# Sorting groups of 4096 edges by merged runs, with row scaling on ScalarE and one-comparison one-hots, in a three-pass graph kernel

## The chip, the cores and the metric

The kernel runs on one core of a Trainium2 chip. The metric is the device time of one execution in microseconds (us), smaller is better. TensorE (PE) multiplies, VectorE (DVE) and ScalarE (ACT) work elementwise, GpSimd (POOL) issues the gathers, SyncE (SP) issues the plain transfers.

## The reference

`x` has 12500 nodes of 96 features; 200000 edges (`src`, `dst`, `weight`, 32 attributes) are sorted by `dst`. A GCN of two layers and one GINE layer follow each other:

```python
# gcn_conv, twice: out[d] = sum over edges (s, d) of norm * (h @ W)[s]
norm = dinv[row] * ew * dinv[col]
out = jax.ops.segment_sum(h[row] * norm[:, None], col, num_segments=n_nodes)
x = x + log_softmax(gcn2(relu(gcn1(relu(layernorm(x))))))
# GINE: message, sum by target, small MLP, batch norm
msg = jax.nn.relu(x[src] + edge_attr @ We + be)
aggr = jax.ops.segment_sum(msg, dst, num_segments=x.shape[0])
```

So there are three passes over all edges (passes 0, 1, 2). Each fetches a row of 96 floats per edge by `src` and adds the rows up by `dst`; passes 0 and 1 weigh each row by the edge's weight, pass 2 adds the attributes' term and takes a ReLU.

## The kernel before, in words

**Steps.** 512 edges (4 per partition, G = 4) are a step; there are NS = 391. Step s uses buffer u = s mod 10 (U = 10), and a loop iteration has 10 steps: 38 iterations (LOOPS) and 11 last steps. A step in pass 0 is: ACT stages the edge's indices and weights (`stage`), POOL issues four gathers of 128 rows from a table in HBM into `rows_g` (`gather`, line 658), DVE makes a one-hot of the targets (`build_hot`: for each of the four columns, `iota == target` times the weight, 128 wide), PE multiplies rows by one-hot into PSUM (`aggregate`, line 1142), and DVE adds the window of 128 nodes into `acc` (`add_window`, line 1582). ACT stages step s + 10 once step s is aggregated.

**Selected rows.** In passes 1 and 2 steps 3, 5, 7, 9 of an iteration (SEL) have no gather. Their edges were sorted by block (`src` mod 100) during pass 0, in groups of 2048 edges, one group per iteration. PE then picks the rows out of a table in SBUF (`tab3`, three bfloat16 parts of 96, so 288 columns): a sorted column of 128 edges spans at most KB = 10 blocks, so `select` multiplies ten `mask`s by ten table columns for each of four columns, 40 matmuls (line 1222). DVE makes the masks (line 1605) and sums the three parts into `rows_g` (`join_rows`, line 1619). Of an iteration's 40 gathers 24 are left. The iteration runs in four segments: `select(i)`, then the aggregations of SEGS[i]. In pass 2 the gathered steps also take an edge term: PE turns the attributes (line 1124) and multiplies them (line 1129), DVE adds (line 1591), ACT takes the ReLU (line 890).

**The sort in pass 0.** For a group of 2048 edges PE and DVE count blocks and ranks (lines 1150 to 1158, 1641 to 1658), DVE makes a permutation `iota_h == rank` of 128x2048 for each of the 16 columns (line 1662), and PE multiplies each by the attributes and the payload in four matmuls of 512 columns (line 1165). These lie in steps 2 to 7 between the aggregations; each engine takes its instructions in the order in which they are written, and waits on semaphores.

## Time and profile before

| | |
|---|---|
| median of 3 runs | 5602.56 us (5595.03 to 5612.93) |
| profiled execution | 5616.2 us, its span 5614.4 us |
| pass 0 | 270 to 2435 us |
| pass 1 | 2541 to 3794 us |
| pass 2 | 3971 to 5455 us |
| mean granted clock of TensorE | 0.855 |
| busy | PE 77%, POOL 67%, DVE 66%, ACT 23% |

The passes' limits are the first gather, the last aggregation and the first and last `select` in the trace. Busy shares are means over passes with different limits, so each pass is read by itself. A DMA_INDIRECT row of POOL is the making of one gather's descriptors. Rows give busy time of a group, the mean length of one instruction, and the engine's idle time before it with what ended it.

### The profile page before, as it was taken

To read this page: it belongs to the slowest core of one execution; us is meant where nothing else is said; L and a number is where in the kernel's file an instruction comes from. 1 tells how busy PE (TensorE), PEld (TensorE's weight loads), DVE (VectorE), ACT (ScalarE), POOL (GpSimd) and SP (SyncE) were. 2 spreads that over 40 slices of the span, in tenths; PEclk is the share of its full clock that TensorE was granted. 3 is DMA by queue.
4 is the path that set the end of the run, shared out by engine and by line. 5 is a ranking of instruction groups with operands and counts; after the bars stand their busy time and mean duration, and the time that the engine had idled before them with its cause. 6 is when DMAs were issued, how large, how long until landed. Compare 5 with 4: busy or idle time off the path is not lost.

```text
span 5614.4 us, 116632 instructions
## 1 busy us (share of the span) xinstructions
PE 4328.9 (77%) x29893; PEld 3358.6 (60%) x29894; DVE 3689.5 (66%) x10748; ACT 1292.0 (23%) x4287; POOL 3768.6 (67%) x3554
## 2 busy tenths in 40 slices
PE   4566666666666666668999999996699999999995
PEld 4444444444444444456777777775577777777773
DVE  3466666665666666647888888886666666666662
ACT  5111111111111111142111111113433333332223
POOL 2377777777777777737777777775666665666663
PEclk6577787777778787859999999996899999999997
DMA  2122222222222222212222222223232322222224
GB/s 54 37 47 46 50 47 47 48 47 48 46 48 46 49 48 49 46 52 52 52 51 51 51 51 51 51 48 111 65 70 65 70 68 66 70 62 67 63 59 109
DMA packets 239972, 316.92 MB, mean 56 GB/s; under 512 B 69263, under 2 KB 175178, under 8 KB 239545
## 3 DMA queue, kind: packets, MB, share of 16 engines
q0 software_dynamic: 111232, 170.85, 15.6%
q1 hardware_dynamic: 128688, 145.48, 8.9%
q8 instruction: 20, 0.33, 0.0%
q14 instruction: 32, 0.26, 0.0%
HBM read 276.92 MB, written 39.15 MB: 56 GB/s over the span
## 4 chain that ended last, share of the span: by engine, by line
PE 60%; DVE 13%; POOL 11%; issue 10%; DVEq 2%; ACT 2%; DMA 1%; POOLq 0%; ACTq 0%; SPq 0%
PE psum L1222 26%; PE psum L1142 15%; POOL rows_g L658 11%; PE psum L1165 7%; PE psum L1129 3%; DVE x_tab L1662 2%; PE psum L1086 2%; PE psum L1150 2%; PE psum L1154 1%; DVE x_tab L1657 1%; DVEq L432 1%; PE psum L1214 1%; PE psum L1289 1%; DMA rows_g<-table,idx 1%; DVE rows_g L1619 1%
## 5 line engine op out<-in xcount | busy, mean ns | idle before, releaser
L658 POOL DMA_INDIRECT rows_g<-table,idx x3476 | 3605.6, 1037 | 1547.3 <-issue 1011.3
L1222 PE MATMUL psum<-x_tab 125*128 x8512 | 1148.9, 289 | 83.9 <-issue 46.2
L1142 PE MATMUL psum<-hot,rows_g 128*96 128x128 f32 x7512 | 1077.4, 297 | 143.5 <-DMA rows_g<-table,idx 70.7
L1142 PEld LDWEIGHTS psum<-hot,rows_g 128*96 128x96 f32 x7512 | 980.8, 181 | 236.4 <-issue 145.8
L1222 PEld LDWEIGHTS psum<-x_tab 125*128 125x128 bf16 x8512 | 827.3, 97 | 393.9 <-issue 135.0
L1165 PE MATMUL psum<-x_tab 128*104 128x512 bf16 x2432 | 614.5, 403 | 534.4 <-DVE x_tab L1662 526.3
L1582 DVE TENSOR_TENSOR acc<-acc,psum 96x128 f32 x1173 | 328.8, 280 | 962.9 <-PE psum L1142 945.2
L791 ACT ACTIVATE attr<-edge 128x12 f32 (+1 forms) x1173 | 243.5, 211 | 2806.3 <-PE psum L1142 2805.6
L1165 PEld LDWEIGHTS psum<-x_tab 128*104 128x104 bf16 x2432 | 303.1, 133 | 780.6 <-ACT x_tab L848 321.9
L1573 DVE TENSOR_SCALAR hot<-iota,attr 128x128 f32<-128x128 f32 x2504 | 686.4, 356 | 7.3 <-ACT acc L785 4.8
L1619 DVE TENSOR_REDUCE rows_g<-psum 128x384 f32<-128x1152 f32 x304 | 412.3, 1356 | 341.2 <-PE psum L1222 336.9
L1605 DVE TENSOR_SCALAR x_tab<-x_tab 125x512 bf16<-125x512 bf16 x2128 | 498.9, 303 | 86.3 <-ACT x_tab L810 43.3
L1222 PE MATMUL psum<-x_tab,x_more 125*128 x3648 | 493.9, 287 | 0.0
L1222 PEld LDWEIGHTS psum<-x_tab,x_more 125*128 125x128 bf16 x3648 | 353.3, 97 | 127.4 <-issue 17.1
L1662 DVE TENSOR_SCALAR x_tab<-x_tab 128x2048 bf16<-128x2048 f16 x608 | 428.1, 755 | 0.2 <-issue 0.2
L890 ACT ACTIVATE rows_g<-rows_g 128x384 f32<-128x384 f32 x391 | 201.1, 514 | 375.5 <-DVE rows_g L1619 211.6
L1142 PE MATMUL psum<-x_more,rows_g 128*96 128x128 f32 x1872 | 258.0, 282 | 27.2 <-DMA rows_g<-table,idx 15.1
L1142 PEld LDWEIGHTS psum<-x_more,rows_g 128*96 128x96 f32 x1872 | 221.5, 166 | 49.6 <-ACT rows_g L890 17.9
L1129 PE MATMUL psum<-we_blk,x_more 128*128 128x384 f32 x478 | 205.4, 512 | 57.2 <-DVE rows_g L1591 56.6
L810 ACT ACTIVATE x_tab<-x_tab,down 125x512 bf16<-125x512 uint16 x304 | 218.6, 719 | 29.8 <-issue 14.8
L1605 DVE TENSOR_SCALAR x_more<-x_tab 125x512 bf16<-125x512 bf16 x912 | 214.1, 300 | 0.0
L1569 DVE TENSOR_TENSOR hot<-iota,attr 128x512 f32<-128x512 f32 x313 | 202.1, 683 | 9.5 <-ACT idx L793 8.4
(255 smaller groups left out, 3692.3 us busy)
## 6 DMA issues: line engine op xcount, KB each, us to landing
rows_g<-table,idx POOLq DMA_INDIRECT x3476, 2.5
x_tab<-sorted_keys SPq DMA_DIRECT2D x304, 125.0 KB
x_more<-in_edge_attr_dram SPq DMA_DIRECT2D x238, 64.0 KB
sorted_attr<-x_tab SPq DMA_DIRECT2D x38, 384.0 KB
x_more<-sorted_attr SPq DMA_DIRECT2D x152, 96.0 KB
table<-x_tab SPq DMA_DIRECT2D x13, 840.0 KB
x_tab<-in_edge_attr_dram SPq DMA_DIRECT2D x38, 256.0 KB, 2.8
x_tab<-in_x_dram SPq DMA_DIRECT2D x2, 4200.0 KB
```

Of the source, the lines that this page charges most:

```text
L658: pool.indirect_dma_start(out=rows_g[u][0:np_, g * F:(g + 1) * F], out_offset=None, in_=table[p], in_offset=bass.IndirectOffsetOnAxis(ap=i ...
L791: last = act.activation(attr[u][0:np_, :], e[:, G:4 * G], ACT.Copy)
L810: act.activation(key_b[i % 2], key_in[i % 2], ACT.Identity, bias=down[0:PN, 0:1]).then_inc(s_kb, 1)
L1129: pe.matmul(ps_e[0:np_, :], eaT[:, 0:np_], we_blk[:, :], start=True, stop=True).then_inc(ring.lin, 1)
L1142: last = pe.matmul(ps_agg[t.b], rows_g[t.u][0:t.np_, g * F:(g + 1) * F], hot[t.h][0:t.np_, g, :], start=g == 0, stop=g == G - 1)
L1165: last = pe.matmul(ps_perm[b], ship[:, c, :], perm[c % 3][:, b * BK:(b + 1) * BK], start=c == 0, stop=c == SC - 1)
L1222: last = pe.matmul(ps_sel[c], mask[i % 2][j][:, c * P:(c + 1) * P], tab3[:, j:J - KB + 1 + j, :, :][:, bass.ds(w[c], 1), :, :].rearrange(" ...
L1573: last = dve.tensor_scalar(hot[t.h][0:np_, g, :], iota[0:np_, 0:W], rel[:, g:g + 1], attr[t.u][0:np_, G + g:G + g + 1], ALU.is_equal, ALU. ...
L1582: dve.tensor_tensor(a, a, ps_agg[t.b], ALU.add).then_inc(fast.added, 1)
L1605: dve.tensor_scalar(mask[i % 2][j], key_b[i % 2], float(j), None, ALU.is_equal).then_inc(s_mask, 1)
L1619: dve.tensor_reduce(rows_g[t.u].rearrange("e (c f) -> e c f", c=G), ps_sel4.rearrange("e c (k f) -> e c f k", k=3), AX.X, ALU.add).then_in ...
L1662: dve.tensor_scalar(perm[c % 3], iota_h, rank[:, c:c + 1], None, ALU.is_equal).then_inc(s_perm, 1)
```

## The change

- **Groups of 4096 edges.** Two iterations (20 steps) sort one group. Its 32 columns are four runs of eight. A run is sorted by 8 permutations of 128x1024, each used as stationary operand by eight matmuls (`permute`); the sorted runs are copied by ACT and then merged by 32 further comparisons of 128x1024, each moved through PE in two matmuls (`merge`). A sorted column then spans at most KB = 6 blocks: `select` has 24 matmuls, and six masks are made for it.
- **Paced permutations.** POOL counts `fast.issue` up before every gather of pass 0; permutation m of step k waits until gather 4 (k + 2) + m is about to be issued.
- **Wider windows.** The targets of a group of 4096 span more nodes: one-hot, aggregation and window of selected steps are 200 wide (WP), 128 for the others.
- **Weights.** In passes 0 and 1 ACT multiplies the rows in place by the weight (`scale_rows`), and the aggregation waits for that.
- **One-hots.** One `tensor_tensor` comparison makes all four columns; in passes 0 and 1 its `iota` lies in PSUM.
- In passes 1 and 2 most one-hots are written behind `join_rows`, and the edge terms stand at other blocks (`EA_AT`). The buffers of one-hots are laid out anew (`hot`, `hot_age`). Ranks of four runs come from one PSUM tile and are split into place and run rank by integer steps (`sort_rank`; a group of 4096 has 25 instructions chained by waits on DVE, a group of 2048 had 13). A branch taken only if a group doesn't fit its window puts the unsorted edges back.

```diff
+    L2, U2, N2, C2, S2 = LOOPS // 2, 2 * U, 2 * NP, 2 * SC, 2 * SE
+    NR = 4
+    RL = C2 // NR
+    RW = RL * P
+    MARGIN = 256
+    MW = NR * P + 2 * MARGIN
+    PT = 4
+    KB = 6
+    WP = 200
+    HP = 4
+    LEAD = 8
...
+            def hot(self, p):
+                if p == 0:
+                    return hot[self.h]
+                if self.sel:
+                    return hot_p[self.i]
+                return (hot_p[0], hot_g[2], hot_p[3] if p == 1 else hot_g[0])[(self.s - LOOPS * U) % 3] if self.rest else hot_g[GAT.index(self.u) % 3]
+
+            def hot_age(self, p):
+                return H if p == 0 else U if self.sel else 3 if self.rest else NG - 2
+
+            def width(self, p):
+                return WP if self.selected(p) else W
+
+            def bank(self, p):
+                return (ps_agg_p if self.selected(p) else ps_agg)[self.b]
...
             def gather(ring, p, s, u, np_, got):
                 pool.wait_ge(ring.staged, p * NS + s + 1)
-                pool.sem_inc(ring.issue, 1)
                 for g in range(G):
+                    if g == 0 or p == 0 and ring is fast:
+                        pool.sem_inc(ring.issue, 1)
...
+            def scale_rows(p, t):
+                if t.selected(p):
+                    act.wait_ge(s_row, t.pi + 2)
+                else:
+                    act.wait_ge(fast_got[t.u], t.got(p))
+                for g in range(G):
+                    r = rows_g[t.u][0:t.np_, g * F:(g + 1) * F]
+                    last = act.activation(r, r, ACT.Copy, scale=attr[t.u][0:t.np_, G + g:G + g + 1])
+                last.then_inc(s_scaled, 1)
...
             def select_pass():
                 def one(it):
                     for i in range(NP):
                         key_ahead(1, it, i)
+                        for k in SEGS[i]:
+                            scale_rows(1, Step(it, k))
                         stage_seg(1, it, i)
...
+                scale_rows(0, Step(0, 0))
+                with act.Fori(0, L2) as it:
+                    for k in range(U2):
                         sort_part(it, k)
-                        stage_fast(0, Step(it, k + U))
+                        scale_rows(0, Step(2 * it, k + 1))
+                        stage_fast(0, Step(2 * it, k + U))
...
-                elif t.selected(p):
-                    pe.wait_ge(s_row, t.pi + 2)
                 else:
-                    pe.wait_ge(fast_got[t.u], t.got(p))
+                    pe.wait_ge(s_scaled, n + 1)
                 for g in range(G):
-                    last = pe.matmul(ps_agg[t.b], rows_g[t.u][0:t.np_, g * F:(g + 1) * F], hot[t.h][0:t.np_, g, :],
+                    last = pe.matmul(t.bank(p), rows_g[t.u][0:t.np_, g * F:(g + 1) * F],
+                                     t.hot(p)[0:t.np_, g, 0:t.width(p)],
...
-                for b in range(4):
-                    last = pe.matmul(ps_perm[b], ship[:, c, :], perm[c % 3][:, b * BK:(b + 1) * BK], start=c == 0, stop=c == SC - 1)
+                    pe.wait_ge(s_keyc, it + 1)
+                if k == 0:
+                    pe.wait_ge(s_run, it * 2 * NR + 2 * r + 1)
+                    for b in range(2):
+                        pe.matmul(bank[4 + b][:, 0:HP * PM], zeros[:, 0:P], zeros[:, 0:HP * PM], start=True, stop=False)
+                pe.wait_ge(s_perm, n + 1)
+                for o in range(RL):
+                    last = pe.matmul(ps_run[o // HP][:, o % HP, :], perm[c % PT][:, o * P:(o + 1) * P], ship[:, c, :],
+                                     start=False, stop=k == RL - 1 and o % HP == HP - 1)
                 last.then_inc(s_permd, 1)
...
+            def merge(it, k, r):
+
+                n = it * 2 * C2 + C2 + k * NR + r
+                t, c = perm[(k * NR + r) % PT], ship2[:, r * RL + k, 0:PF]
+                lo = MARGIN if k == 0 else 0
+                hi = MW - MARGIN if k == RL - 1 else MW
+                if k == 0 and r == 0:
+                    pe.wait_ge(s_run, it * 2 * NR + 2 * NR + 1)
+                if r == 0:
+                    pe.wait_ge(s_eao, it * (RL + 1) + k + 1)
+                pe.wait_ge(s_perm, n + 1)
+                pe.matmul(ps_merge[k % 2][:, lo:BK], c, t[:, lo:BK], start=k == 0 and r == 0, stop=r == NR - 1)
+                pe.matmul(ps_merge[(k + 1) % 2][:, 0:hi - BK], c, t[:, BK:hi], start=r == 0,
+                          stop=k == RL - 1 and r == NR - 1).then_inc(s_permd, 1)
...
-            EA_AT = ({2: 0, 5: 1, 8: 2}, {5: 3}, {5: 4}, {5: 5})
+            EA_AT = ({1: 0, 3: 1, 5: 2}, {3: 3}, {3: 4}, {3: 5})
...
                 dve.wait_ge(fast.staged, n + 1)
-                dve.wait_ge(fast.agg, n + 1 + U - H)
+                dve.wait_ge(fast.agg, n + 1 + U - t.hot_age(p))
                 rel = attr[t.u][0:np_, 0:G]
-                if p == 2:
-                    last = dve.tensor_tensor(hot[t.h][0:np_, :, :], iota[0:np_, 0:W].unsqueeze(1).to_broadcast([np_, G, W]),
-                                             rel.unsqueeze(2).to_broadcast([np_, G, W]), ALU.is_equal)
-                else:
-                    for g in range(G):
-                        last = dve.tensor_scalar(hot[t.h][0:np_, g, :], iota[0:np_, 0:W], rel[:, g:g + 1],
-                                                 attr[t.u][0:np_, G + g:G + g + 1], ALU.is_equal, ALU.mult)
+                last = dve.tensor_tensor(h[0:np_, :, 0:w], (iota if p == 2 else ps_iota)[0:np_, 0:w].unsqueeze(1).to_broadcast([np_, G, w]),
+                                         rel.unsqueeze(2).to_broadcast([np_, G, w]), ALU.is_equal)
                 last.then_inc(fast.hot, 1)
...
-            def sort_perm(it, c):
-                dve.wait_ge(s_permd, SC * it + c + 1)
-                dve.tensor_scalar(perm[c % 3], iota_h, rank[:, c:c + 1], None, ALU.is_equal).then_inc(s_perm, 1)
...
+            def sort_perm(it, k, m):
+                q = (k - PERM_AT) * NR + m
+                dve.wait_ge(s_permd, it * 2 * C2 + q + 1)
+                dve.wait_ge(fast.issue, (it * U2 + k) * G + LEAD + m + 1)
+                if k < MERGE_AT:
+                    at = rank[:, q:q + 1]
+                else:
+                    at = place[:, m * RL + k - MERGE_AT:m * RL + k - MERGE_AT + 1]
+                dve.tensor_scalar(perm[q % PT], iota_h, at, None, ALU.is_equal).then_inc(s_perm, 1)
...
+                with dve.Fori(0, L2) as it:
                     links[0] = 0
-                    w = windows(dve, mybir.EngineType.DVE, it * U, U, win_row)
-                    for k in range(U):
+                    for k in range(U2):
+                        if k % U == 0:
+                            w = windows(dve, mybir.EngineType.DVE, it * U2 + k, U, win_row)
+                        now, ahead = Step(2 * it, k), Step(2 * it, k + LA)
                         if k == 0:
                             sort_blocks(it)
-                        build_hot(0, Step(it, k + LA))
-                        if k == 9:
+                        if PERM_AT <= k < MERGE_AT + RL:
+                            if k == MERGE_AT:
+                                sort_places(it)
+                            sort_perm(it, k, 0)
+                            if k > PERM_AT:
+                                add_window(0, Step(2 * it, k - 1), at)
+                            sort_perm(it, k, 1)
+                            build_hot(0, ahead)
+                            sort_perm(it, k, 2)
+                            sort_perm(it, k, 3)
+                            at = w[k % U] * AL
+                            continue
...
-                        for k in HOTS[i]:
+                        early = 1 if edge_terms[2:] else 0
+                        for k in HOTS[i][:early]:
                             build_hot(p, Step(it, k))
                         for t in edge_terms[2:]:
                             add_edge_term(fast, t.gi, t.got(2), t.u, EP)
                         join_rows(p, Step(it, SEL[i]))
+                        for k in HOTS[i][early:]:
```

DVE in pass 0, before: one step in the middle of a group's permutations (`x_tab<-x_tab 128x2048` is a permutation, `hot<-iota,attr` a one-hot, `acc<-acc,psum` a window).

```order
L1661 REGISTER_ALU
L1662 TENSOR_SCALAR x_tab<-x_tab 128x2048 [waits permutation_used]
L1661 REGISTER_ALU
L1662 TENSOR_SCALAR x_tab<-x_tab 128x2048 [waits permutation_used]
L1565 REGISTER_ALU
L1573 TENSOR_SCALAR hot<-iota,attr 128x128 [waits fast_agg,fast_staged]
L1573 TENSOR_SCALAR hot<-iota,attr 128x128 x3
L1579 REGISTER_ALU
L1582 ISA [waits fast_added,fast_agg]
L1582 TENSOR_TENSOR acc<-acc,psum 96x128
```

DVE in pass 0, after, the same place: `x_tab<-x_tab 128x1024` is a permutation.

```order
L1768 REGISTER_ALU
L1769 ISA [waits permutation_used]
L1774 TENSOR_SCALAR x_tab<-x_tab 128x1024 [waits fast_issue]
L1672 REGISTER_ALU
L1675 ISA [waits fast_added,fast_agg]
L1675 TENSOR_TENSOR acc<-acc,psum 96x128
L1768 REGISTER_ALU
L1769 REGISTER_ALU [waits permutation_used]
L1774 TENSOR_SCALAR x_tab<-x_tab 128x1024 [waits fast_issue]
L1663 REGISTER_ALU
L1666 TENSOR_TENSOR hot<-psum,attr 128x512 [waits fast_agg,fast_staged]
```

The three permutations in a row became four of half the width, each behind a wait for POOL's count (`fast_issue`), with the window's addition and the one-hot, now one instruction, between them.

PE in pass 0, before: two permutations and the next aggregation (`psum<-x_tab 104x512` and `psum<-hot,rows_g`).

```order
L1161 REGISTER_ALU
L1165 MATMUL psum<-x_tab 104x512 [waits permutation_ready]
L1165 MATMUL psum<-x_tab 104x512 x3
L1133 REGISTER_ALU
L1142 MATMUL psum<-x_more,rows_g 96x128 [waits fast_gathered4,fast_added,fast_hot]
L1142 MATMUL psum<-x_more,rows_g 96x128 x3
```

PE in pass 0, after, the same place.

```order
L1252 REGISTER_ALU
L1254 MATMUL psum<-x_tab 128x106 [waits permutation_ready]
L1254 MATMUL psum<-x_tab 128x106 x7
L1203 REGISTER_ALU
L1210 MATMUL psum<-x_more,rows_g 96x128 [waits rows_scaled,fast_added,fast_hot]
L1210 MATMUL psum<-x_more,rows_g 96x128 x3
```

Each permutation went from four matmuls of 512 columns with the same stationary operand to eight of 106 columns with eight different ones, and the aggregation waits for ACT's scaling instead of the gather.

## Rows read from the trace of the kernel before

**Rows 1.** The span in 40 slices (page, part 2): busy tenths, granted clock.

```profile
POOL 2377777777777777737777777775666665666663
PEclk6577787777778787859999999996899999999997
```

**Rows 2.** The three passes: busy us (x instructions) by engine, PEclk, DMA.

```profile
270.00:2435.00 2165.00, 1394.83 (x7627) 1033.56 (x7626) 1345.78 (x3653) 297.75 (x1153) 1685.83 (x1564) 0.76 0.21 47
...
2541.00:3794.00 1253.00, 1163.91 (x9098) 919.47 (x9099) 1025.86 (x3560) 203.94 (x756) 887.13 (x904) 0.99 0.25 51
...
3971.00:5455.00 1484.00, 1385.87 (x10389) 1080.88 (x10388) 989.69 (x2742) 487.96 (x1588) 916.53 (x907) 1.00 0.28 66
```

**Rows 3.** Groups of instructions, 400 to 2350 us (pass 0).

```profile
L658 POOL DMA_INDIRECT rows_g<-table,idx x1412 | 1520.5, 1077 | 430.5 <-issue 421.9 <-ACT idx L793 8.5
L1165 PE MATMUL psum<-x_tab 128*104 128x512 bf16 x2240 | 562.8, 402 | 492.5 <-DVE x_tab L1662 492.5
...
L1662 DVE TENSOR_SCALAR x_tab<-x_tab 128x2048 bf16<-128x2048 f16 x560 | 394.3, 755 | 0.0
...
L1154 PE MATMUL psum<-x_more,x_tab 128*128 128x100 bf16 x576 | 111.8, 363 | 0.0
...
L1652 DVE TENSOR_TENSOR x_tab<-x_tab 128x512 f32<-128x512 f32 x72 | 49.9, 693 | 4.4
...
L1641 DVE TENSOR_TENSOR x_more<-x_more 128x1600 bf16<-128x1600 bf16 x36 | 36.2, 1005 | 89.7 <-issue 89.7
```

**Rows 4.** POOL in order of time, 702 to 711.9 us: start, length.

```profile
702.21 0.95 POOL L658 DMA_INDIRECT rows_g<-table,idx  x1 [0.30 <-issue]
703.46 1.35 POOL L658 DMA_INDIRECT rows_g<-table,idx  x1 [0.30 <-issue]
...
707.69 2.56 POOL L658 DMA_INDIRECT rows_g<-table,idx  x1 [0.30 <-issue]
```

**Rows 5.** DVE in order of time, 702 to 711.9 us.

```profile
703.25 2.08 DVE L1662 TENSOR_SCALAR x_tab<-x_tab 128x2048 bf16<-128x2048 f16 x3
...
708.07 2.07 DVE L1662 TENSOR_SCALAR x_tab<-x_tab 128x2048 bf16<-128x2048 f16 x3
```

**Rows 6.** Groups of instructions, 2600 to 3750 us (pass 1).

```profile
L658 POOL DMA_INDIRECT rows_g<-table,idx x835 | 814.4, 975 | 336.4 <-issue 228.9 <-ACT idx L793 105.3 <-ACT attr L791 2.1
...
L1573 DVE TENSOR_SCALAR hot<-iota,attr 128x128 f32<-128x128 f32 x1116 | 301.2, 362 | 0.0
L1142 PE MATMUL psum<-hot,rows_g 128*96 128x128 f32 x2224 | 280.2, 277 | 39.8 <-issue 38.7
...
L1605 DVE TENSOR_SCALAR x_tab<-x_tab 125x512 bf16<-125x512 bf16 x980 | 227.3, 300 | 68.8 <-issue 38.6 <-ACT x_tab L810 30.2
```

**Rows 7.** Groups of instructions, 4050 to 5400 us (pass 2).

```profile
L658 POOL DMA_INDIRECT rows_g<-table,idx x827 | 833.4, 1008 | 518.3 <-ACT idx L793 301.5 <-issue 216.8
L1222 PE MATMUL psum<-x_tab 125*128 x3864 | 519.1, 286 | 0.0
...
L1222 PE MATMUL psum<-x_tab,x_more 125*128 x1654 | 225.3, 286 | 0.0
...
L1569 DVE TENSOR_TENSOR hot<-iota,attr 128x512 f32<-128x512 f32 x277 | 177.5, 679 | 0.0
```

**Rows 8.** Waits, 4050 to 5400 us: total us, times, longest.

```profile
POOL rows_g L658 <- ACT idx L793: 301.5, 118, 7.7
DVE rows_g L1619 <- PE psum L1222: 267.9, 137, 2.3
```

**Rows 9.** Groups of instructions, whole span.

```profile
L1656 DVE TENSOR_TENSOR x_tab<-x_more,psum 128x1600 f32<-128x1600 bf16 x38 | 68.8, 1809 | 0.0
...
L938 ACT ACTIVATE x_tab<-x_tab,dinv 125x96 f32<-125x96 f32 x52 | 15.2, 363 | 15.6 <-DVE x_tab L1893 15.6
```

**Rows 10.** All engines in order of time, 5026 to 5030 us.

```profile
5026.27 1.28 DVE L1569 TENSOR_TENSOR hot<-iota,attr 128x512 f32<-128x512 f32 x2
...
5027.07 1.30 POOL L658 DMA_INDIRECT rows_g<-table,idx  x1 [0.30 <-issue]
```

More of the change, by code:

```diff
@@ L190, in build_gnn @@
         edge2 = at_x.take(RS * 4 * G).rearrange("p (s k) -> p s k", k=4 * G)
-        iota_h = at_x.take(SE, F16)
-        perm = [at_x.take(SE, BF16) for _ in range(3)]
+        iota_h = at_x.take(RW, F16)
+        perm = [at_x.take(RW, BF16) for _ in range(PT)]
         pay = at_x.take(RC * 8, BF16).rearrange("p (t k) -> p t k", k=8)
         lower, ones_b, ident_b = [at_x.take(P, BF16) for _ in range(3)]
-        before = at_x.take(J)
+        before = at_x.take((2 * NR - 1) * J)
         first_row = at_x.take(P)
+        ones_row = at_x.take(P)[0:1, :]
@@ L203, in build_gnn @@
+        ea_raw = at_tab.take(C2 * KE).rearrange("p (c k) -> p c k", k=KE)
+        ship, ship2 = [at_tab.take(C2 * PM, BF16).rearrange("p (c k) -> p c k", k=PM) for _ in range(2)]
+        ea_out = at_tab.take(S2, BF16)
         key_T = at_tab.take(P, U16)
-        tot_sb = at_tab.take(P)
-        dupes, rank, blk_s, dst_s, wgt_s, start_s, key_s, miss, rel_s, far_s = [at_tab.take(SC) for _ in range(10)]
-        same = at_tab.take(SC * SC).rearrange("p (c d) -> p c d", d=SC)
+        dupes, rank, place, blk_s, dst_s, wgt_s, start_s, key_s, miss, rel_s, far_s = [at_tab.take(C2) for _ in range(11)]
@@ L207, in build_gnn @@
+        both_i, one_i = [at_tab.take(C2, I32) for _ in range(2)]
+        same = at_tab.take(C2 * RL).rearrange("p (r c d) -> p r c d", r=NR, c=RL)
         at_low = Place(x_more_t, 0, 10 * P)
-        blk = at_low.take(J * SC, BF16).rearrange("p (j c) -> p j c", c=SC)
         blk_b = at_low.take(RC, BF16)
-        tri = at_low.take(SC * SC, BF16).rearrange("p (c d) -> p c d", d=SC)
+        tri = at_low.take(RL * RL, BF16).rearrange("p (c d) -> p c d", d=RL)
         at_top = Place(x_more_t, 14 * P, 2 * JC * F)
-        iota_jc = at_top.take(J * SC, BF16).rearrange("p (j c) -> p j c", c=SC)
+        iota_j = at_top.take(J, BF16)
@@ L258, in build_gnn @@
         ps_agg = [bank[k][0:F, 0:W] for k in range(2)]
+        ps_agg_p = [bank[k][0:F, 0:WP] for k in range(2)]
         ps_e = bank[2][:, 0:G * F]
@@ L833, in select_pass, with copy_run @@
                 one(LAST)
[L834 to L837 removed]
+                for t in last_steps():
+                    scale_rows(1, t)
+                    if t.s - LOOPS * U + U < REST:
+                        stage_fast(1, Step(LOOPS, t.s - LOOPS * U + U))
+            def copy_run(it, r):
+                act.wait_ge(s_permd, PT + it * 2 * C2 + (r + 1) * RL)
+                for b in range(2):
+                    c = r * RL + b * HP
+                    act.activation(ship2[:, c:c + HP, :], ps_run[b], ACT.Copy).then_inc(s_run, 1)
@@ L1898, in _, with put_back @@
             if_far(dve, lambda: sweep(0))
+            def put_back():
+                e = [edge[:, 0:RS, k * G:(k + 1) * G] for k in range(4)]
+                dve.wait_ge(s_back, 48)
+                dve.tensor_copy(e[0], back_i[0])
+                dve.memset(e[1], BIG)
+                dve.tensor_copy(e[2], back_w)
+                dve.tensor_copy(e[3], back_i[1]).then_inc(s_backed, 1)
+            if_far(dve, put_back)
             dve.wait_ge(s_eas, 16 * (LOOPS + 1))
-            dve.wait_ge(s_keyd, 16 * (LOOPS + 1))
+            dve.wait_ge(s_keyd, 16 * (L2 + 1))
             dve.wait_ge(s_par, 16 * 11)
```

393 lines of the change are left out of this document (216 added, 177 removed).

## The prediction

> **What bounds the kernel now.** I read the slices first, then the passes by windows, then each pass's groups, waits and order of time. The slices show three stretches: POOL busy at seven tenths at a TensorE clock of 0.5 to 0.8, then POOL at seven with the clock full, then at six [rows 1]. The windows give them numbers [rows 2]. An iteration takes 2165 / 1564 x 40 = 55.4 us in pass 0 (1564 gathers, 40 to an iteration), 1253 / 38 = 32.97 in pass 1 and 1484 / 38 = 39.05 in pass 2.
>
> Pass 0 is POOL's. Its idle time is 430.5 us before 1412 gathers, 0.30 each, all but 8.5 us of it issue: nobody makes it wait [rows 3]. An undisturbed gather has 0.95 us and 0.30 before it [rows 4], a floor of 1.25; here the mean is (1520.5 + 430.5) / 1412 = 1.38. The 0.13 between them comes from DVE. The gather at 703.46 took 1.35 us, that at 707.69 2.56 [rows 4]; beside the first, three permutations began 0.21 earlier, beside the second, 0.38 later, and its end (710.25) is theirs (710.14) [rows 5]. So a gather needs something that a permutation holds, early and once more late, and three without a gap shut it out to the end.
>
> Pass 1 is PE's, narrowly: 1163.9 of 1253 us busy, clock 0.99 [rows 2]; 24 gathers at 1.25 are 30.0 us of 32.97, so POOL's floor lies 3 us below. Pass 2 is PE's too: 1385.9 of 1484 us, clock 1.00 [rows 2]; POOL needs 24 x (1.008 + 0.30) = 31.4 of 39.05 [rows 7], and spends 301.5 us waiting for ACT's staging, which waits for aggregated steps. DVE's wait is for `select` itself, 267.9 us [rows 8].
>
> **The change, part by part.** *Select.* Four selected steps have 96 matmuls for 160. One costs (519.1 + 225.3) / 5518 = 0.135 us [rows 7], so 64 fewer are -8.64 us of PE an iteration. Against that the 16 aggregating matmuls of selected steps are 200 columns wide for 128: one of 128 takes 280.2 / 2224 = 0.126 [rows 6], in proportion +0.07 each, +1.1 us; since a four-byte product may take more than its share and the zeroing and windows grow too, I book 2.3, double. PE's need falls to 26.6 in pass 1 and 32.7 in pass 2.
>
> *Pass 1* then meets POOL. As gathers go there now, 24 x (0.975 + 0.30) = 30.6 [rows 6]; with 0.2 for a late first gather I take 30.8. Bounds: 30.0, and 32.97 if a chain of waits keeps the old period. DVE loses 16 masks at 0.23 (227.3 / 980), -3.7 us, and forty one-hots of 301.2 / 1116 = 0.27, 10.8 us, for six in one comparison of 512 columns (0.64 by [rows 7]) and four of 800, which from 0.64 and the 1.81 of a 1600-column one [rows 9] is 0.95: 7.7. It has 1025.9 / 38 = 27.0 now [rows 2, 6], some 20 of 30.8 then: no bound. -2.17 x 38 = **-83**.
>
> *Pass 2*: PE 32.7, POOL 31.4, 1.3 apart, so either will now and then wait for the other, and the shorter first `select` covers less of the edge terms behind it. I take 33.6, 0.9 above PE; bounds 32.7 and 36, the latter if the 2.3 us of longest wait between POOL or DVE and PE [rows 8] come once an iteration and an aggregation's chain once more. -5.45 x 38 = **-207**. All its one-hots stay two-SBUF comparisons; one at 5026.27 overlapped a gather that took 1.30 [rows 10], 0.35 over the floor. Four of an iteration's ten grow from 0.64 to 0.95, at most +0.3 us each on POOL, 32.6: still PE's.
>
> The Trainium skill (SBUF — State Buffer, "SBUF: two separate sides") says that DVE and GpSimd share a port pair under an exclusive lock for a whole instruction, and counts a DVE op with two SBUF inputs among the holders only against a GpSimd op that reads SBUF; its trap about DMAs from POOL's queue names only the fast two-port modes. By the trap alone pass 2's one-hots would hold nothing, POOL would need 30.0, and pass 2 would be 32.7, the sum 34 us lower. The gather of 1.30 us beside a two-input comparison [rows 10] speaks for the first form, in which a PSUM input frees the one-hots of passes 0 and 1.
>
> *Scaling by ACT*: four activations of 128x96 a step, 0.363 us each by the nearest row [rows 9], 1.45 us. Pass 0: 391 x 1.45 = 567 on top of 298 busy of 2165 [rows 2]; pass 1 the same on 204 of 1253, so about 770 of 1170: hidden. Queued behind a waiting `scale_rows` is the staging of a step ten ahead, and behind that POOL. The scaling of step k+1 waits for its gather, staging then has some eight steps (each 4 x 1.25 = 5 us) in hand: no wait as long as ACT's 1.45 and PE stay within 5 us. Cost 0; without that cover 1.45 us x 10 an iteration. Aggregation later by 1.45 us is covered by the same ring.
>
> *Pass 0's permutations.* 608 of 128x2048 become 1216 of 128x1024, 64 to 80 gathers. Between 0.300 us for 512 columns [rows 6] and 0.755 for 2048 [rows 3] lies 0.45. Each is let go when POOL counts up in the 0.30 before a gather, so I place it like the one at 703.25: from 0.21 before the gather's start to 0.24 behind it. How long does the gather wait? At 703.46 the first of the three (2.08 / 3 = 0.69) ended 0.48 after the gather's start and cost it 0.40, so it wanted the port at 0.08. Here it would wait 0.24 - 0.08 = 0.16 at most, nothing if the release lets DVE start and end a little sooner. No row has such a release; I take half, 0.08: 64 x 0.08 = 5.1 us. Groups no longer come three in a row, so nothing of 2.56 is left. The one-hots read PSUM: 0, bound above by the 0.35 of [rows 10] for 20 of them, 7 us. The sort's other wide work (some four of the 0.69 of L1652, two of the 1.0 of L1641 [rows 3], a part of it beside no gather's need) and late gathers after a loop's turn: I take 4 us, between 1.5 and 6. Sum: 100 + 4 + 5.1 = 109.1 for 80 gathers against 110.7 today, -1.6 x 19 = **-30**. Bounds: 101.5, and 116 with 0.16 for each permutation and 6 for the rest (20 one-hots left at 0).
>
> PE in pass 0: a permutation step has 32 products of 106 columns with their own weights, 0.194 us each at the lower clock (111.8 / 576, L1154) [rows 3], 6.2 us, which is more than a step's 5.0 to 5.5 before the aggregation is added; at the full clock about half. Before, 16 permutations in six steps took 2.7 x 4 x 0.25 (562.8 / 2240) = 2.7 us a step. So PE gets near its limit where the clock stays at its lower level, 8 of 20 steps; eight steps of lag at most 1.5 to 2 us each, 12 to 16 us, are covered by the ring's eight steps of 5 us, and the next twelve lighter steps win it back. Merges have two products of up to 512 columns: less than before. Cost 0.
>
> *The sum.* -30 - 83 - 207 = -320 from the profiled 5616.2 is 5296. The median of the runs is 13.6 under the profiled time, so I predict **5282 us**.
>
> **Rivals.** (A, the forecast, 0.62: 5170 to 5370.)
> (B) Pass 2 stops at 36 by its chain of waits and pass 0 gains nothing: -83 - 116 = -199, 5404; if the scaling's 1.45 us enters a period of pass 1 too, 5460. For it: PE and POOL lie close, and [rows 8] has such waits; against: these come from PE's load. 5370 to 5520, 0.17.
> (C) Collisions vanish in pass 0 (101.5) and the others reach 30.3 and 32.7: -175 - 101 - 241 = -517, 5086. 5060 to 5170, 0.10.
> (D) Slower: the pacing makes every permutation meet its gather as at 703.46. At 0.40 each pass 0 is 100 + 4 + 25.6 = 129.6, +359, 5671 with the other gains kept. It decides from (290 / 19 + 110.7 - 104) / 64 = 0.34 us a permutation. For it: pacing puts all 64 where a collision costs; against: 0.45 is shorter than 0.69. 0.04.
> (E) Slower: TensorE's clock. PE, now busy 93% in passes 1 and 2 at 0.99 and 1.00, was busy 64% in pass 0 at 0.76 [rows 2], between its levels of 1.2 and 2.4 GHz. After the change it idles 14% of pass 1. At a mean grant of 0.8 pass 1 takes 26.6 / 0.8 = 33.3 and pass 2 40.9: +11 + 70 - 30, 5654. It decides from 0.81. Against: pass 2, with the larger lever, stays full. 0.05.
> The Trainium skill (TensorE: Matmul & The Clock Gate, Part 1) has the throttled state as the default and activity as what releases it; this is the rule behind E, and rows 2 agree in direction.
> (F) The selected part doesn't shrink, as with a fallback to unsorted edges taken: about 5570 to 5620, 0.02; it would show as more work between passes.
>
> **How the numbers follow.** A measurement of this kernel tells about 0.3% (17 us) from no change. The range 5150 to 5440 holds A, most of B and a little of C, about 0.8. Faster: A, B, C and half of F, 0.90; same 0.02; slower: D, E with the lower part left for mishaps of a new sort, 0.08.
>
> **What would show it.** In the changed profile: pass 1 at 1170 us with POOL's idle time before gathers almost all issue; pass 2 near 1280 with PE still over 90% busy; pass 0 at 2135, its gathers a mean 1.06 us, few over 1.5; `select` at 24 matmuls; the granted clock in passes 1 and 2 at 0.95 or more; ACT's scaling near 0.36 us and no gather waiting for staging in pass 0. Wrong would be: gathers of 1.3 us in the paced steps (D), a clock under 0.9 in pass 1 (E), POOL waiting for staging in pass 0 (PE or ACT behind), or pass 2's waits of PE for `rows_g` above 1 us an iteration (B).

## The result and the profile after

The changed kernel takes 5427.09 us (median of 4 runs, 5423.47 to 5428.28) against 5605.27 us on the same chip: a ratio of 0.968, 95% interval 0.967 to 0.970. It is faster by 178 us; 5282 was predicted. The range of 5150 to 5440 holds the time, by 13 us; it lies outside the forecast's own stretch (A, 5170 to 5370) and inside that of rival B (5370 to 5520). More than 40% of the forecast gain is missing, and the passes tell where. The three passes by windows, with the limits taken as in [rows 2] (busy us and instructions by engine, then granted clock, DMA share, GB/s):

```profile
271.00:2418.00 2147.00, 1338.42 (x11448) 1061.62 (x11449) 1239.70 (x2822) 756.09 (x2771) 1666.23 (x1564) 0.78 0.22 48
2524.00:3655.00 1131.00, 963.39 (x6665) 780.94 (x6666) 776.86 (x1812) 602.14 (x2270) 855.18 (x894) 0.94 0.28 56
3849.00:5263.00 1414.00, 1184.39 (x7954) 911.29 (x7953) 914.23 (x2135) 500.20 (x1588) 904.50 (x905) 0.99 0.30 69
```

| | before | forecast | after |
|---|---|---|---|
| pass 0 | 2165 | -30 | 2147 (-18) |
| pass 1, first to last select | 1253 | -83 | 1131 (-122) |
| pass 1, last select to last aggregation | 41 | 0 | 57 (+16) |
| pass 2 | 1484 | -207 | 1414 (-70) |
| all else | | 0 | +6 |
| span | 5614.4 | | 5426.4 (-188) |

Pass 0 gave 18 of the 30 us forecast, pass 1 more than forecast, pass 2 a third. In the slices POOL is at seven tenths in passes 0 and 1, as before (its issue gaps do not count as busy), and in pass 2 at six tenths, as before: there it is not the limit.

```profile
POOL 2377777777777777764777777775666666666663
PEclk6577877787777877766999999995799999999997
```

Groups of instructions, 400 to 2350 us (pass 0) of the changed kernel, against [rows 3]:

```profile
L699 POOL DMA_INDIRECT rows_g<-table,idx x1424 | 1517.4, 1066 | 434.0 <-issue 427.9 <-ACT idx L836 6.1
L1774 DVE TENSOR_SCALAR x_tab<-x_tab 128x1024 bf16<-128x1024 f16 x1147 | 537.6, 492 | 344.1 <-PE psum L1270 236.1 <-PE psum L1254 74.1 <-POOLq L698 32.0
L873 ACT ACTIVATE rows_g<-rows_g,attr 128x96 f32<-128x96 f32 x1422 | 414.5, 363 | 744.2 <-DMA rows_g<-table,idx 743.7
```

A gather's mean is 1.066 us (1.06 was forecast), a permutation's 0.49 (0.45), a scaling's 0.363 (0.363). Of DVE's waits before permutations only 32.0 us are for POOL's count; 310 are for PE. POOL still waits for nobody: 6.1 us for ACT's staging, the rest is issue. But "few over 1.5" did not come: counted in the trace, 138 of these gathers take over 1.5 us, for 58 before, and 31 over 2 us, for 56.

Groups, 2600 to 3600 us (pass 1), against [rows 6]:

```profile
L699 POOL DMA_INDIRECT rows_g<-table,idx x794 | 758.8, 956 | 242.0 <-issue 234.0 <-ACT attr L834 5.8 <-ACT idx L836 2.1
```

The gather fell from 0.975 to 0.956 us and its waits for ACT from 107.4 us in 835 gathers to 7.9 in 794: 24 x (0.956 + 0.295 of issue) = 30.0, and the iteration takes 1131 / 38 = 29.8 (a few of its gathers were issued ahead of the first `select`). Pass 1 is at POOL's floor.

Groups, 3950 to 5200 us (pass 2), against [rows 7], and waits in the same stretch, against [rows 8]:

```profile
L699 POOL DMA_INDIRECT rows_g<-table,idx x807 | 805.4, 998 | 445.7 <-issue 235.4 <-ACT idx L836 210.3
```

```profile
DVE rows_g L1712 <- PE psum L1327: 237.6, 129, 4.2
POOL rows_g L699 <- ACT idx L836: 210.3, 37, 7.0
PE psum L1210 <- DVE acc L1675: 98.8, 67, 2.3
DVE acc L1675 <- PE psum L1210: 81.3, 67, 1.9
```

Here the period is 1414 / 38 = 37.2 us, PE is busy 31.2 of them, and POOL still waits for staging. A wait has grown that was small before: PE's for a window that DVE has still to add, 98.8 us. In the kernel before, in the stretch of [rows 8], it was

```profile
PE psum L1142 <- DVE acc L1582: 16.4, 23, 0.7
```

In order of time it looks like this (PE, DVE, POOL in the first segment of an iteration, loads left out):

```profile
4460.92 1.91 PE L1210 MATMUL psum<-x_more,rows_g 128*96 128x128 f32 x16
...
4461.21 1.36 DVE L1712 TENSOR_REDUCE rows_g<-psum 128x384 f32<-128x1152 f32 x1 [1.76 <-PE psum L1327]
...
4462.48 0.98 DVE L1666 TENSOR_TENSOR hot<-iota,attr 128x800 f32<-128x800 f32 x1
...
4463.28 0.99 POOL L699 DMA_INDIRECT rows_g<-table,idx  x1 [6.32 <-ACT idx L836]
4463.38 0.69 DVE L1666 TENSOR_TENSOR x_more<-iota,attr 128x512 f32<-128x512 f32 x1
4463.98 0.73 DVE L1690 TENSOR_REDUCE nmax<-x_more 125x96 f32 x4
...
4464.62 0.27 DVE L1675 TENSOR_TENSOR acc<-acc,psum 96x128 f32 x1
...
4465.13 2.02 PE L1210 MATMUL psum<-hot,rows_g 128*96 128x128 f32 x8 [2.30 <-DVE acc L1675]
```

Steps 0 and 1 are aggregated at 4462.8. Step 2 needs step 0's bank, whose window DVE adds at 4464.6, because the join and two one-hots stand ahead of it in DVE's order, and the row maxima of the output's softmax, which 25 of the 38 iterations have. PE waits 2.30 us; the next eight records of 128 columns (one step's four products, two records each) then take 2.02 us where eight otherwise take 1.04; the last section shows why. Staging waits for PE, and POOL's gather had waited 6.32 us for staging.

### The profile page after: what moved, and what is told of

Read it like the earlier page. It is cut to its first block, busy times and chain, and to the rows that moved or that the text cites. A ratio compares the mean times of both kernels' runs of the same rounds, so it can differ in the third digit from the quotient of the medians.

```text
span 5426.4 us, 112908 instructions
## 1 busy us (share of the span) xinstructions
PE 3877.0 (71%) x28867; PEld 3083.6 (57%) x28868; DVE 3257.8 (60%) x7538; ACT 2176.8 (40%) x7472; POOL 3717.5 (69%) x3554
## 3 DMA queue, kind: packets, MB, share of 16 engines
q14 instruction: 124, 1.02, 0.1%
## 4 chain that ended last, share of the span: by engine, by line
POOL 39%; PE 25%; issue 20%; DVE 8%; DMA 2%; ACT 2%; DVEq 1%; POOLq 1%; ACTq 0%; SPq 0%
POOL rows_g L699 39%; PE psum L1327 9%; PE psum L1210 7%; PE psum L1199 3%; DVE x_more L1666 2%; PE psum L1156 2%; DMA rows_g<-table,idx 2%; PE psum L1386 1%; DVE x_tab L1721 1%; PE psum L1194 1%; DVE acc L1675 1%; DVE hot L1666 1%; PE psum L1319 1%; POOLq L698 1%; DVE rows_g L1712 0%
## 5 line engine op out<-in xcount | busy, mean ns | idle before, releaser
L873 ACT ACTIVATE rows_g<-rows_g,attr 128x96 f32<-128x96 f32 x3128 | 898.4, 362 | 1072.1 <-DMA rows_g<-table,idx 1004.2
L1210 PE MATMUL psum<-hot,rows_g 128*96 128x128 f32 (+1 forms) x4456 | 741.7, 319 | 527.9 <-ACT rows_g L873 424.8
L1210 PEld LDWEIGHTS psum<-hot,rows_g 128*96 128x96 f32 x4456 | 637.9, 189 | 618.7 <-issue 524.2
L1774 DVE TENSOR_SCALAR x_tab<-x_tab 128x1024 bf16<-128x1024 f16 x1216 | 570.0, 492 | 365.5 <-PE psum L1270 250.3
L1210 PE MATMUL psum<-x_more,rows_g 128*96 128x128 f32 (+1 forms) x4296 | 636.2, 298 | 112.6 <-ACT rows_g L873 112.5
L1675 DVE TENSOR_TENSOR acc<-acc,psum 96x128 f32 (+1 forms) x1173 | 349.0, 298 | 568.1 <-PE psum L1210 498.9
L1210 PEld LDWEIGHTS psum<-x_more,rows_g 128*96 128x96 f32 x4296 | 569.3, 168 | 150.9 <-issue 127.5
L1666 DVE TENSOR_TENSOR hot<-psum,attr 128x512 f32<-128x512 f32 (+2 forms) x435 | 303.2, 704 | 1.7 <-issue 1.3
L1254 PE MATMUL psum<-x_tab 128*128 128x106 bf16 x4864 | 293.3, 226 | 0.0
L1269 PE MATMUL psum<-x_tab 128*104 128x512 bf16 (+1 forms) x608 | 262.6, 436 | 37.7 <-DVE x_tab L1774 36.7
L1270 PE MATMUL psum<-x_tab 128*104 128x512 bf16 (+1 forms) x608 | 262.4, 432 | 0.0
```

The lines of the kernel that those rows point to most:

```text
L873: last = act.activation(r, r, ACT.Copy, scale=attr[t.u][0:t.np_, G + g:G + g + 1])
L1210: last = pe.matmul(t.bank(p), rows_g[t.u][0:t.np_, g * F:(g + 1) * F], t.hot(p)[0:t.np_, g, 0:t.width(p)], start=g == 0, stop=g == G - 1)
L1254: last = pe.matmul(ps_run[o // HP][:, o % HP, :], perm[c % PT][:, o * P:(o + 1) * P], ship[:, c, :], start=False, stop=k == RL - 1 and o % ...
L1269: pe.matmul(ps_merge[k % 2][:, lo:BK], c, t[:, lo:BK], start=k == 0 and r == 0, stop=r == NR - 1)
L1666: last = dve.tensor_tensor(h[0:np_, :, 0:w], (iota if p == 2 else ps_iota)[0:np_, 0:w].unsqueeze(1).to_broadcast([np_, G, w]), rel.unsquee ...
L1675: dve.tensor_tensor(a, a, t.bank(p), ALU.add).then_inc(fast.added, 1)
```

## The experiments

Theory 1: in pass 2 DVE's order sets the period. The one-hots, which the change wrote behind `join_rows`, hold back the window additions, PE waits for a bank, and POOL for what PE has not yet aggregated. Theory 2: the period comes instead from the coupling with POOL's staging or from the chain of edge terms behind a shorter first `select`. Runs were made on several chips. Beside the last four, as beside the result, the kernel before takes 5595 to 5613 us; on the two chips of the first eight it takes 6956 and 7050 us. The last section says what those two chips show; here their stretches are compared only with one another, and the verdicts rest on the others. Stretches with the same code tell how far a difference can be trusted: on the two chips passes 0 and 1 differ by up to 29 us from run to run (pass 0: 2874, 2886, 2888 and 2901; pass 1: 1615, 1621 and 1643), on the others by 4 (pass 0: 2147 and 2151; pass 1: 1131 twice).

**One-hots ahead of the join, pass 2.** All of `HOTS` but step 4's, whose buffer is in use until step 0 is aggregated.

```diff
-                        early = 1 if edge_terms[2:] else 0
+                        early = (2, 3, 2, 2)[i] if p == 2 else 0
-                return H if p == 0 else U if self.sel else 3 if self.rest else NG - 2
+                return H if p == 0 else U if self.sel else 3 if self.rest else 5 if self.u == 1 else NG - 2
```

> Pass 2 alone is changed: the one-hots that the changed kernel writes behind join_rows stand ahead of it again, all but that of step 4, whose buffer is still in use. Theory 1 (DVE's order: behind the join the one-hots hold back the window additions, and TensorE waits for a bank before the third aggregation of a segment): TensorE's idle time of about 6 us per iteration of pass 2 falls by 2 to 3 us, the period from 37.3 to about 35, the whole run by 75 to 110 us. Theory 2 (the coupling with POOL's staging or the edge terms' chain sets the period): the run moves by less than 20 us.

6923.8 us, 0.995 (0.993 to 0.998) of the kernel before there. Pass 2 (first to last select) takes 1766 us against 1892 and 1896 in the two runs below on this chip that leave it alone: about -128.

**First edge terms one block later, pass 2.** `EA_AT` for the first `select`: `{1: 0, 3: 1, 5: 2}` to `{2: 0, 4: 1, 5: 2}`.

> In pass 2 the first two edge terms of an iteration stand behind two and four blocks of the first select, for one and three. Theory 1 (the first edge term waits for ACT's copy, about 1 us an iteration, because fewer products stand ahead of it): the wait of 0.95 us per iteration falls to about 0.3 and the run by up to 25 us. Theory 2 (the chain of edge terms ends later and the third aggregation waits for it): no change or up to 20 us slower.

7041.8 us, ratio 1.012 (1.008 to 1.017); pass 2 takes 1880 us, beside 1892 and 1896 without the edit. If it helps, it is by no more than about 15 us, which is within what same code differs by here. Against the second half of theory 2 this is evidence from this chip alone; the edit was not run on a chip of the other kind.

**No pacing, pass 0.**

```diff
-                dve.wait_ge(fast.issue, (it * U2 + k) * G + LEAD + m + 1)
```

> Pass 0 alone: the permutations no longer wait for POOL's count, only for their buffer. Theory 1 (spacing them keeps gathers from being shut out for long): pass 0 gets 20 to 60 us longer, with gathers of 2 us and more again. Theory 2 (most permutations are late for the count anyway and wait for TensorE): no difference beyond 15 us. Theory 3 (the count puts each permutation where a gather starts and costs more than it saves): 15 to 40 us shorter.

6972.1 us, ratio 1.002 (1.000 to 1.004); pass 0 takes 2791 us beside 2840 and 2856 with pacing. That is 49 to 65 us less, theory 3 and more than its 15 to 40; the other kind of chip says the opposite, below.

**iota in SBUF, passes 0 and 1.** `(iota if p == 2 else ps_iota)` becomes `iota`.

> The comparisons of passes 0 and 1 read iota from SBUF instead of PSUM. Theory 1 (a comparison with both inputs in SBUF holds gathers back, one with an input in PSUM does not): 0.2 to 0.35 us for each of 391 one-hots of pass 0 and most of the 391 of pass 1, where gathers set the period: together 100 to 250 us slower. Theory 2 (the source does not matter): within 15 us.

7142.6 us, ratio 1.026 (1.022 to 1.030); pass 0 takes 2968 us, 112 to 128 longer than in the two runs above that leave it alone. In pass 1, where POOL waits for others on this chip, it costs nothing (1548 us against 1584 to 1590 in the three runs above).

**The changed kernel itself on such a chip.**

> The changed kernel as it is, to stand beside the others on the same chip. Every theory: 0.968 of the kernel before if the chip is like the first one; on a chip like that of the first four experiments, on which the kernel before takes 6956 us, nothing is known.

7173.6 us: 1.017 of the kernel before there (1.012 to 1.021). What is 3.2% faster on one chip is about 1.7% slower on another. Its passes take 2901, 1643 and 1928 us.

**The one-hots again, beside it.**

> The edit of the first experiment once more, beside the changed kernel itself. Theory 1 (one-hots behind the join hold back the window additions, and TensorE the third aggregation): pass 2 shorter by 75 to 110 us than in the changed kernel, the period about 35 us, TensorE's wait inside the first segment from 1.8 us to under 0.5. Theory 2 (POOL's staging or the edge terms' chain sets the period): within 20 us.

7021.9 us, ratio 0.996 (0.994 to 0.998); pass 2 takes 1777 us for 1928: theory 1 forecast 75 to 110 less, and it is 151.

**Windows of steps 0 and 1 ahead of the late one-hot and the row maxima.** To the edit above comes, with the same two additions left out of the next segment:

```diff
                         join_rows(p, Step(it, SEL[i]))
+                        if p == 2 and i == 0:
+                            for k in (0, 1):
+                                add_window(p, Step(it, k), at[k])
```

> As the one before, and in the first segment of pass 2 the window additions of steps 0 and 1 stand right behind the join, ahead of the late one-hot and the row maxima. Theory 1: a further 5 to 30 us. Theory 2: no difference.

7029.7 us, ratio 0.998 (0.995 to 1.000); pass 2 takes 1778 us. No further gain on this chip.

**Four products of a select twice.** The third block's loop over the columns runs twice; the selected rows count that block double.

> The four products of the third block of every select are issued twice, 16 more an iteration, about 2.15 us of TensorE, in passes 1 and 2; the selected rows come out changed by it. If pass 1 is POOL's (its period of 29.9 us is 24 gathers at 1.25) it stays within 10 us, since TensorE idles 4.3 us an iteration. Pass 2: if TensorE's own work with a fixed chain of waits sets the period, it takes 2.15 us more an iteration, 80 us in all; if POOL, DVE or a loop of waits beside it sets the period, under 20 us.

7295.4 us, ratio 1.034 (1.031 to 1.037). Against the changed kernel on this chip pass 1 takes 36 us more (58 and 65 more than the two runs above, which have the same pass 1), pass 2 101 more. So PE's path counts in both passes here; that its late signals (last section) make it so is likely and was not tested.

**Three edits, one to a pass (k1).** No pacing in pass 0, the products twice in pass 1, one-hots ahead in pass 2.

> Three edits in one kernel, one to a pass, each read in its own stretch of the trace. Pass 0: permutations without POOL's count. Pass 1: four products of every select issued twice, 16 more an iteration (the selected rows come out changed). Pass 2: one-hots ahead of the join. The stretches of the changed kernel are 2147, 1131 and 1414 us. On a chip on which TensorE's semaphores arrive at once, as in the trace of the changed kernel: pass 0 by theory 1 (spacing helps) 20 to 60 us longer, by theory 2 (TensorE sets most permutations' time) within 15; pass 1 within 10 us if POOL's floor of 24 gathers at 1.25 us sets its period, up to 80 us longer if TensorE does; pass 2 shorter by 75 to 110 us if DVE's order sets its period, within 20 us if POOL's staging or the edge terms do. On a chip like those of the experiments so far, pass 2 about 135 us shorter and pass 0 about 50 us shorter than the changed kernel there.

5380.0 us; ratio 0.960 (0.959 to 0.962). By windows:

```profile
271.00:2449.00 2178.00, 1380.26 (x11451) 1090.21 (x11450) 1234.18 (x2822) 756.84 (x2770) 1697.57 (x1564) 0.76 0.20 47
2554.00:3692.00 1138.00, 1005.04 (x7268) 831.05 (x7269) 781.72 (x1814) 601.90 (x2272) 859.97 (x900) 0.95 0.27 56
3878.00:5207.00 1329.00, 1175.54 (x7955) 908.85 (x7954) 918.82 (x2135) 492.04 (x1588) 910.93 (x902) 0.98 0.32 74
```

Pass 0 is 31 us longer: spacing the permutations saves 31 / 19 = 1.6 us per 80 gathers. Gathers over 2 us are 65 here (400 to 2350 us), for 31 with pacing. Pass 1 took 42 us more of PE (1005 for 963) and only 7 us more of time, so POOL's floor sets it. Pass 2 lost 85 us: theory 1. PE's wait for a window, 2.9 us an iteration in the changed kernel (98.8 us in 1250), is down to 1.1 (3950 to 5150 us):

```profile
PE psum L1210 <- DVE acc L1676: 37.8, 34, 1.3
```

**Three edits (k2).** iota in SBUF in pass 0, a scaling of one column of four in pass 1 (three columns stay without weights), the products twice in pass 2.

> Three edits, one to a pass. Pass 0: iota of the one-hots in SBUF instead of PSUM. If two inputs in SBUF hold gathers back, 20 one-hots for 80 gathers at 0.2 to 0.35 us each make pass 0 75 to 130 us longer than 2147; if not, within 15 us. Pass 1: ACT scales only one of a step's four columns (the other three stay without their weights). If the scaling is hidden, the pass stays at 1131 within 10 us; if ACT's 1.45 us a step is on the path, up to 100 us shorter. Pass 2: the four products of one block of every select are issued twice, +2.15 us of TensorE an iteration: 80 us longer than 1414 if TensorE's work plus a fixed chain sets the period, under 25 if the extra products only fill its 6 us of idle time.

5545.3 us; ratio 0.990 (0.989 to 0.992).

```profile
273.00:2491.00 2218.00, 1366.29 (x11438) 1083.22 (x11436) 1237.29 (x2820) 752.72 (x2768) 1738.49 (x1564) 0.77 0.21 46
2597.00:3727.00 1130.00, 966.11 (x6664) 780.20 (x6663) 777.10 (x1812) 313.90 (x1134) 854.91 (x893) 0.94 0.28 56
3920.00:5383.00 1463.00, 1257.84 (x8564) 978.11 (x8563) 915.32 (x2136) 500.39 (x1588) 907.12 (x907) 0.98 0.30 67
```

Pass 0: +71 us (75 to 130 if such comparisons hold gathers back), and POOL's busy time +72: all of it is in the gathers. The comparison itself lasts as long as before, 0.68 us. Pass 1: ACT's work about halved, 602 to 314 us, and the time the same. Pass 2: PE +73, time +49. That lies between the two values expected: two thirds of PE's added work are on the path and one third fits into its idle time, which a loop of waits between PE and DVE would explain.

**Three edits (k3).** A scaling of one column in pass 0 (three columns without weights), iota in SBUF in pass 1, one-hots ahead and windows first in pass 2.

> Three edits, one to a pass. Pass 0: ACT scales only one of a step's four columns (the other three stay without their weights); if the scaling is hidden the pass stays at 2147 us within 10, if the aggregation's lag by it is on the path up to 60 us shorter. Pass 1: iota of the one-hots in SBUF; by the 0.19 us that each cost in pass 0 of the kernel before this one, 10 an iteration make 1.9 us, 72 us longer than 1131, if they meet gathers there as often; if not, within 15. Pass 2: one-hots ahead of the join, and in its first segment the window additions of steps 0 and 1 right behind the join, ahead of the late one-hot and the row maxima; against 1414 us shorter by 85 as without the second part, and by a further 10 to 40 if TensorE's remaining 1.1 us wait for a window there is what the period still has from DVE's order.

5370.2 us; ratio 0.960 (0.957 to 0.962).

```profile
270.00:2431.00 2161.00, 1333.80 (x11454) 1060.71 (x11452) 1235.19 (x2823) 447.32 (x1598) 1680.63 (x1564) 0.78 0.21 48
2535.00:3725.00 1190.00, 984.92 (x6661) 797.53 (x6661) 777.69 (x1812) 600.82 (x2268) 916.18 (x894) 0.92 0.25 53
3921.00:5198.00 1277.00, 1160.73 (x7949) 900.85 (x7948) 912.80 (x2134) 492.15 (x1588) 982.01 (x901) 1.00 0.33 77
```

Pass 0 is not shorter with a quarter of the scaling (+14 us, all in POOL's busy time; why is open). Pass 1: +59 us, POOL +61. Pass 2: -137 us, so the windows' place is worth 52 beyond the one-hots' 85. 72 us were expected for pass 1, 10 to 40 for the second part of pass 2.

**The last edit alone.**

> The changed kernel with the pass 2 edit of the last experiment alone (one-hots ahead of the join, the window additions of steps 0 and 1 ahead of the late one-hot and the row maxima). If the 136 us that pass 2 lost there come from DVE's order and nothing of them from the other two edits, the whole run takes 5427 - 136, about 5290 us, 0.944 of the kernel before; if pass 1 or 0 had a part in it, 5310 to 5340.

5288.1 us (5282.8 to 5301.0); ratio 0.9425 (0.941 to 0.944): 5.7% faster than before, 2.6% beyond the change, with instructions moved on DVE and one count of a wait. About 5290 was expected if the passes of the runs with three edits can be read each by itself; they can. Pass 2 by windows, then groups and waits, 3950 to 5050 us:

```profile
3849.00:5125.00 1276.00, 1161.85 (x7956) 901.19 (x7955) 915.21 (x2135) 492.24 (x1588) 981.93 (x901) 1.00 0.33 77
```

```profile
L699 POOL DMA_INDIRECT rows_g<-table,idx x783 | 851.1, 1087 | 249.9 <-issue 223.1 <-ACT idx L836 26.8
```

```profile
DVE rows_g L1712 <- PE psum L1327: 136.4, 125, 1.7
POOL rows_g L699 <- ACT idx L836: 26.8, 51, 2.9
```

In order of time, PE and DVE at the same place as above:

```profile
4471.18 1.36 DVE L1712 TENSOR_REDUCE rows_g<-psum 128x384 f32<-128x1152 f32 x1 [1.56 <-PE psum L1327]
4472.45 0.27 DVE L1675 TENSOR_TENSOR acc<-acc,psum 96x128 f32 x1
...
4472.96 1.11 PE L1210 MATMUL psum<-hot,rows_g 128*96 128x128 f32 x8
```

The window follows the join at once, PE goes on without a wait, and its wait for windows has left the list of waits. POOL's wait for staging fell from 210.3 us to 26.8, though nothing of POOL or ACT was moved: it came from DVE's order too. Gathers now take 1.087 us: 24 x (1.087 + 0.285 of issue) = 32.9 of the period of 33.6 (1276 / 38). Pass 2 is then POOL's, and for both halves of theory 2 at most the last 0.7 us are left. What its gathers meet are one-hots with both inputs in SBUF, now three in a row in the second segment:

```profile
4476.35 3.43 POOL L699 DMA_INDIRECT rows_g<-table,idx  x1 [0.30 <-issue]
...
4476.48 2.48 DVE L1666 TENSOR_TENSOR x_more<-iota,attr 128x800 f32<-128x800 f32 x3
```

21 gathers of this stretch take over 3 us, none did in the changed kernel. Spreading the three, or their `iota` in PSUM, was not tried in pass 2.

## Why the prediction was right, and where not

- **Direction and range** held; the gain forecast as 320 us was 188 by the profiles, and the range held by 13 us. The time fell where rival B (0.17) had put it. B named the right pass and the nearest mechanism, a stop of pass 2 at 36 us by a chain of waits (it was 37.2), but had pass 0 gain nothing and pass 1 no more than 83. Rivals C to F did not happen.
- **Pass 2 (failed: "I take 33.6, 0.9 above PE").** The 0.9 was for edge terms that a shorter `select` uncovers and for PE and POOL waiting for one another. The loss came from an edit for which the sum had no term: the one-hots moved behind the join. Moving them back, all but step 4's, took 85 us off. Adding the windows of steps 0 and 1 ahead of step 4's one-hot and of the row maxima took another 52, to 33.6 us. The 52 are not all a loss by the change: the row maxima stood ahead of these windows in the kernel before too. How they divide between the one-hot and the maxima was not tried. That 33.6 equals the forecast is half luck: it was to be PE's 32.7 and 0.9 of waits, and it is POOL's 32.9 and 0.7.
- **PE's need** was put too high. The sum took 8.64 off the iteration's whole time (32.97 and 39.05 us), idle time included, and called the rest PE's. From the busy time (30.6 and 36.5) the same terms give 24.3 and 30.1; 25.4 and 31.2 were measured. 64 products less saved 7.7 us in pass 2, not 8.64: `select` is busy 809.3 us before and 517.8 after, so one product takes 0.142 us for 0.133.
- **The width** was booked at 2.3 us an iteration, as double the share by columns, and took 1.7 to 2.3: right, but not by a surcharge. A four-byte product leaves two matmul records, eight for a step's four products, so the prediction's 0.126 is half a product and its single share half of the share by columns. In order of time, pass 2 of the changed kernel, one step of 200 columns and one of 128:

```profile
4472.32 1.52 PE L1210 MATMUL psum<-hot,rows_g 128*96 128x200 f32 x8
...
4473.68 1.04 PE L1210 MATMUL psum<-x_more,rows_g 128*96 128x128 f32 x8
```

  That is +0.06 a record, 1.9 us for the 32 records of an iteration. By windows with all aggregations of pass 2 (before; changed; last kernel) it is 74 us or 2.0 an iteration, and 1.7 in the last kernel:

```profile
3971.00:5455.00 1484.00, 372.38 (x3019) 342.02 (x3020) 1.00 0.28 66
...
3849.00:5263.00 1414.00, 446.83 (x3017) 405.01 (x3018) 0.99 0.30 69
...
3849.00:5125.00 1276.00, 435.92 (x3017) 401.92 (x3018) 1.00 0.33 77
```

- **Pass 1 (-83, measured -122)**: the step "24 x (0.975 + 0.30) = 30.6 [...] with 0.2" kept today's collisions. The comparisons read PSUM now: 0.956 and a period of 29.8. With iota in SBUF the gather takes 1.022 us and the pass 59 us more. 16 us come back behind the last select, since POOL no longer runs ahead: its last 44 gathers need 44 x 1.25 = 55 us.
- **Pass 0 (-30, measured -18)**: 2147 x 80 / 1564 = 109.8 us for 80 gathers against the forecast 109.1. A permutation of 0.49 us and one-hots from PSUM at nothing held. But the mechanism held only in part, and the near sum is in part luck. The forecast let every permutation go by POOL's count, just before a gather, and had no group of them left. In the trace DVE waits 22 times for the count before a permutation and 204 times for PE (400 to 2350 us); late ones follow closely, and 138 gathers are over 1.5 us. The count still pays, by the 31 us of its removal. What the sum booked at 5.1 us for 64 permutations was not measured by itself. The one-hots at nothing matter more than all of this: with iota in SBUF 71 us come back, more than pass 0 gained. PE was no danger: a permutation's product of 106 columns, booked at 0.194 us, has 293.3 us of busy time for 4864 of them in the profile, 0.06 each.
- **Scaling at no cost**: with ACT's work cut to about a half pass 1 takes the same time, and pass 0 is not shorter.
- **The port rule** (Trainium skill, SBUF — State Buffer, "SBUF: two separate sides"): two runs agree with its first form, +71 and +59 us when the comparison's second input moved from PSUM to SBUF. The trap, which names fast two-port modes alone, says too little here: the comparison takes 0.68 us with its iota in either place, so no faster mode came in with the move.
- **Clock**: pass 1's grant fell from 0.99 to 0.94 while PE's busy share went from 93% to 85%. It cost nothing there, since POOL sets the time; rival E would have needed 0.81.

## What to carry to other kernels

When a change moves an instruction on an engine that works in order, price it by what stands behind it and who waits for that, even if what moved is short: here one-hots of 0.7 and 1.0 us ahead of a window addition of 0.3 us took back at least 85 us. Put releases (a bank, a buffer) ahead of work that is only needed later: that gave 52 us more. When gathers set the pace, keep one input of VectorE's two-input operations in PSUM: it was worth 71 and 59 us here. And start a sum from an engine's busy time, not from the period, which has its waits in it.
